# A four-stage block on one core: places of work chosen anew, own places for the first and last tile times, first layer and attention turns in column groups

## The reference

```python
x = layernorm(x + attention(x))      # 16 heads of 16, one shared key and value head, softmax over all 512
x = layernorm(x + ffn(x))            # 256 -> 1024 -> 256, weights ternary, exact gelu
x = layernorm(x + state_space(x))    # norm, B, cumulative sum with decay A, C, then the recurrence, then out_w
x = layernorm(x + linear(x))         # both operands quantised to fp6 in blocks of 32, 256 -> 256

def step(h, xt):                     # the recurrence, one step for each of 512 positions
    cat = concatenate([xt, h])
    ff1, ff2 = tanh(cat @ ff1_w.T + ff1_b), tanh(cat @ ff2_w.T + ff2_b)
    t_i = sigmoid((cat @ ta_w.T + ta_b) * 0.1 + (cat @ tb_w.T + tb_b))
    return ff1 * (1 - t_i) + t_i * ff2
```

## Time and profile before

| | before |
|---|---|
| median of 3 runs | 1768.9 us (1768.15 to 1773.33) |
| the profiled execution, its own time | 1771.39 us |
| its span | 1769.6 us |
| PE busy | 1637.5 us, 93% |
| DVE busy | 1343.4 us, 76% |
| ACT busy | 1293.2 us, 73% |
| POOL busy | 1104.3 us, 62% |
| matmuls | 35371 |
| PE's instruction queue | 280 packets, 4.59 MB |

### The profile page before, as it was taken

The page is one execution under the profiler, slowest core; times in us unless marked ns, Lnnn a source line. Parts: engine busy times, 40 slices in busy tenths (PEclk is TensorE's granted clock), DMA queues, the critical chain, the costliest instruction groups (busy, mean ns, idle before and its releaser), DMA issues.

```text
span 1769.6 us, 84556 instructions
## 1 busy us (share of the span) xinstructions
PE 1637.5 (93%) x35371; PEld 1189.0 (67%) x35371; DVE 1343.4 (76%) x2605; ACT 1293.2 (73%) x2601; POOL 1104.3 (62%) x3392
## 2 busy tenths in 40 slices
PE   5768999999999999999999999999999999999865
PEld 4535667677777777677777777777777767776643
...
GB/s 239 203 93 54 60 58 62 74 72 69 51 72 73 73 66 58 67 73 72 70 61 62 74 72 69 61 62 74 71 71 61 62 71 71 73 58 32 18 29 20
DMA packets 133765, 125.18 MB, mean 71 GB/s; under 512 B 18965, under 2 KB 130633, under 8 KB 133385
## 3 DMA queue, kind: packets, MB, share of 16 engines
...
...
## 4 chain that ended last, share of the span: by engine, by line
PE 53%; POOL 15%; ACT 10%; issue 8%; DVE 4%; DMA 4%; SPq 4%; POOLq 0%; DVEq 0%; ACTq 0%
PE value_bank L772 11%; PE gen_bank L910 8%; PE score_banks L750 7%; PE gen_bank L598 6%; PE max_banks L590 6%; PE gate_bank L803 5%; ACT L1130 4%; ACT probs L1130 3%; PE gen_bank L819 3%; PE gate_bank L598 2%; POOL square L1613 2%; POOL rstd L1598 2%; DMA key_pieces<-khalf 2%; POOL diff L1717 2%; POOL hseq L1722 2%
## 5 line engine op out<-in xcount | busy, mean ns | idle before, releaser
L1186 DVE TENSOR_REDUCE nmax<-max_banks 128x2 f32<-128x1024 f32 x512 | 622.5, 1216 | 65.3 <-PE max_banks L592 61.3
L1130 ACT ACTIVATE probs<-score_banks 128x1024 f32<-128x1024 f32 x512 | 525.0, 1025 | 112.3 <-PE score_banks L752 96.3
L772 PE MATMUL value_bank<-probs,vaug 128*32 128x128 f32 x8192 | 327.3, 278 | 1.1 <-issue 1.1
L772 PEld LDWEIGHTS value_bank<-probs,vaug 128*32 128x32 f32 x8192 | 205.5, 110 | 90.6 <-issue 79.7
L590 PE MATMUL max_banks<-kaug,qaug 62*128 62x512 f32 x512 | 238.7, 466 | 24.8 <-DVE nmax L1186 15.7
L750 PE MATMUL score_banks<-qaug,kaug 64*128 64x512 f32 x512 | 237.6, 464 | 12.4 <-ACT probs L1130 7.8
L1717 POOL TENSOR_TENSOR diff<-gates 128x16 f32<-128x16 f32 x472 | 114.2, 242 | 212.3 <-ACT gates L1135 205.1
L592 PE MATMUL max_banks<-kaug,qaug 62*128 62x512 f32 x512 | 239.2, 467 | 0.4 <-issue 0.4
L752 PE MATMUL score_banks<-qaug,kaug 64*128 64x512 f32 x512 | 237.6, 464 | 0.0
L1135 ACT ACTIVATE gates<-gate_bank 128x48 f32<-128x48 f32 x472 | 99.0, 210 | 167.6 <-PE gate_bank L803 167.2
L803 PEld LDWEIGHTS gate_bank<-hseq,ghT 128*32 128x32 f32 x11328 | 159.1, 112 | 81.3 <-POOL hseq L1722 57.4
(11 more groups left out here) (234 smaller groups left out, 3540.6 us busy)
## 6 DMA issues: line engine op xcount, KB each, us to landing
qstage<-qhalf SPq DMA_DIRECT2D x384, 128.0 KB
qstage<-qhalf SPq DMA_DIRECT2D x128, 112.0 KB
...
qaug<-nmT SPq DMA_DIRECT2D x256, 8.0 KB, 1.8
```

Source lines behind the costliest of these rows:

```text
L772: last = pe.matmul(value_bank[32 * g:32 * g + 32, :].rearrange("p (k t) -> p k t", k=HG)[:, :, u * BLOCK_POS:(u + 1) * BLOCK_POS], vaug[:, ...
L1130: act.activation(probs[:, beat % 2, :, :], score_banks[:, :, :], ACT.Exp).then_inc(exp_done, 1)
L1186: dve.tensor_reduce(nmax[:, m % 2, at:at + 9:8], max_banks[:, :, :], AX_X, ALU.max, negate=True).then_inc(max_taken, 1)
```

## The change

1. All slots of a steady tile time are other ones. On PE the order becomes: VALUES0, Q, STEP0, SCORES0, PAIR0, F2_0 to F2_7, TURND, SCORES1, PAIR1, XT, OT, STEP1, LAST, VALUES1, ATT, STEP2, PAIR2, SCORES2, PROJ, VALUES2, STEP3, SCORES3, PAIR3, VALUES3, OUT, STEP4, SCORES4, PAIR4, TURNX, VALUES4, SCORES5, VALUES5, STEP5, B, SCORES6, PAIR5, NM, X1T, STEP6, VALUES6, SCORES7, PAIR6, VALUES7, STEP7, FFN1A, FFN1B, PAIR7, INPUT (for the next tile time). On ACT: TANH0, Q, OT, EXP0, TURND, XT, TANH1, EXP1, ATT, TANH2, EXP2, TANH3, EXP3, TANH4, EXP4, X1, TURNX, EXP5, TANH5, EXP6, X1T, TANH6, X4, X2, EXP7, TANH7, GELUA, GELUB, Q8. On POOL HLOB stands ahead of XD, where it stood behind it.
2. Tile times -2 to 5 have places of their own (`OWN_AT`), and so has tile time 64 (`LAST_AT`). `tile_at`, `beat_at` and `times_of_uses` look there first.
3. `TAIL` and `TAIL_SSM` have other steps for X3B, QMAX, QSCALE, QIN, Q8, LN4, X4 and XN.
4. `QUARTERED` names the pieces whose matmuls are written in column groups. INPUT, LAST, Q, OUT, PROJ and B were so before. New are FFN1A and FFN1B (48 matmuls of 128 columns become 192 of 32) and ATT (2 transposes become 16 matmuls of 32 columns against the identity, written through `turned_block`).

The diff, cut to its core:

```diff
-PE_AT = dict(INPUT=0, F2_0=275, F2_1=280, F2_2=285, F2_3=285, F2_4=286, F2_5=288, F2_6=299, F2_7=302, TURND=279, LAST=322, XT=50, Q=12, OUT=128, OT=65, ATT=73, PROJ=90, TURNX=149, B=160, X1T=217, NM=204, FFN1A=247, FFN1B=249)
-ACT_AT = dict(OT=44, TURND=339, XT=104, Q=29, Q8=253, TURNX=196, ATT=145, X1T=230, GELUA=238, GELUB=239, X1=194, X2=178, X4=496)
-DVE_AT = dict(Q=23, X4R=362, X2R=52, OT=62, X3R=171, X3=239, QUANT=240, XN=148, LN1=157, BS=190, SCAN=236, ORDER=182, X1P=216, HLOA=240, NM=216)
-POOL_AT = dict(LN4=418, LN3=97, LN2=6, LNI=8, QIN=192, X2S=77, XD=214, X3B=193, LN1=15, X1B=116, STATES=165, HLOB=219)
-SP_AT = dict(MOVE=15, X2F=200, STORE=89, OUTST=406, XLD=59, NMPLACE=95)
+PE_AT = dict(INPUT=-2, F2_0=274, F2_1=275, F2_2=278, F2_3=278, F2_4=296, F2_5=297, F2_6=299, F2_7=304, TURND=309, LAST=336, XT=63, Q=8, OUT=134, OT=69, ATT=87, PROJ=100, TURNX=173, B=213, X1T=221, NM=217, FFN1A=240, FFN1B=247)
+ACT_AT = dict(OT=43, TURND=307, XT=51, Q=41, Q8=239, TURNX=158, ATT=99, X1T=193, GELUA=224, GELUB=236, X1=151, X2=202, X4=455)
+DVE_AT = dict(Q=27, X4R=371, X2R=85, OT=97, X3R=189, X3=205, QUANT=252, XN=141, LN1=145, BS=215, SCAN=238, ORDER=203, X1P=234, HLOA=260, NM=220)
+POOL_AT = dict(LN4=384, LN3=101, LN2=45, LNI=61, QIN=201, X2S=204, XD=222, X3B=200, LN1=96, X1B=217, STATES=154, HLOB=204)
+SP_AT = dict(MOVE=34, X2F=66, STORE=108, OUTST=365, XLD=46, NMPLACE=71)
 BEAT_AT = dict(
-    SCORES=(19, 61, 89, 107, 137, 157, 178, 231),
-    PAIR=(18, 55, 87, 102, 140, 202, 236, 250),
-    VALUES=(11, 68, 100, 128, 151, 157, 224, 252),
-    STEP=(15, 51, 72, 93, 135, 156, 166, 229),
-    EXP=(86, 121, 165, 181, 186, 227, 228, 236),
-    TANH=(46, 90, 125, 170, 181, 196, 227, 235),
-    MAX=(17, 26, 60, 107, 160, 190, 213, 233),
-    MIX=(3, 4, 12, 13, 20, 34, 96, 157),
+    SCORES=(14, 61, 99, 113, 154, 185, 216, 230),
+    PAIR=(14, 62, 97, 128, 168, 217, 230, 254),
+    VALUES=(3, 87, 111, 130, 180, 203, 227, 240),
+    STEP=(10, 74, 94, 112, 143, 209, 223, 240),
+    EXP=(49, 97, 121, 132, 142, 168, 179, 210),
+    TANH=(34, 66, 101, 128, 137, 174, 198, 224),
+    MAX=(15, 42, 96, 129, 165, 203, 216, 245),
+    MIX=(3, 61, 72, 80, 97, 109, 132, 133),
 )
-TAIL = dict(OUT=0, X3R=0, LN3=0, STATS3=1, X3=3, X3B=4, QMAX=4, QSCALE=5, QIN=6, Q8=7, XD=8, TURN=9, COPY=9, LAST0=10, LAST1=11, X4R=11, STATS4=12, LN4=12, X4=14, INPUT=1)
-TAIL_SSM = dict(F2=0, X2R=0, LN2=0, X2=2, X2S=2, XN=4, TURN=4, COPY=4, B=5, BS=5, SCAN=6)
+OWN_AT = {
...
+    -1: dict(
+        PE=dict(NM=142),
+        DVE=dict(NM=183),
+        SP=dict(NMPLACE=190),
+        BEAT=dict(PAIR=(-1, -1, -1, -1, -1, 36, 197, 211), MAX=(-1, -1, -1, -1, -1, -1, 12, 221)),
+    ),
...
+    5: dict(
+        PE=dict(INPUT=247, F2_0=80, F2_1=81, F2_2=83, F2_3=122, F2_4=124, F2_5=124, F2_6=126, F2_7=129, XT=140, Q=13, OT=140, ATT=154, PROJ=173, TURNX=190, B=219, X1T=206, NM=231, FFN1A=233, FFN1B=245),
+        ACT=dict(OT=13, XT=85, Q=13, TURNX=148, ATT=89, X1T=186, GELUA=238, GELUB=246, X1=125, X2=234),
+        DVE=dict(Q=51, X2R=82, OT=91, XN=113, LN1=130, BS=160, SCAN=216, ORDER=157, X1P=173, HLOA=26, NM=206),
+        POOL=dict(LN2=23, LNI=23, X2S=107, LN1=38, X1B=106, STATES=108, HLOB=248),
+        SP=dict(MOVE=1, STORE=18, XLD=4, NMPLACE=2),
+        BEAT=dict(SCORES=(22, 134, 141, 170, 184, 203, 219, 230), PAIR=(16, 136, 161, 179, 204, 225, 245, 246), VALUES=(13, 142, 160, 176, 189, 205, 223, 234), EXP=(17, 35, 51, 109, 111, 148, 200, 234), MAX=(39, 74, 103, 112, 142, 149, 201, 219)),
...
+LAST_AT = dict(
+    PE=dict(INPUT=254, F2_0=18, F2_1=19, F2_2=20, F2_3=23, F2_4=40, F2_5=41, F2_6=43, F2_7=48, TURND=53, LAST=80, OUT=134, OT=69, ATT=87, PROJ=100, TURNX=177, B=213, X1T=221, FFN1A=240, FFN1B=247),
+    ACT=dict(OT=42, TURND=90, Q8=239, TURNX=156, ATT=100, X1T=193, GELUA=224, GELUB=228, X1=136, X2=202, X4=199),
+    DVE=dict(X4R=100, X2R=70, OT=89, X3R=189, X3=205, QUANT=252, XN=146, LN1=145, BS=204, SCAN=238, X1P=194, HLOA=4),
+    POOL=dict(LN4=120, LN3=101, LN2=45, LNI=61, QIN=171, X2S=204, XD=222, X3B=215, LN1=96, X1B=213, STATES=212, HLOB=204),
+    SP=dict(X2F=154, STORE=156, OUTST=153),
+    BEAT=dict(VALUES=(3, 87, 101, 120, 170, 183, 202, 226), STEP=(0, 64, 89, 112, 121, 182, 221, 238), TANH=(24, 61, 101, 118, 122, 141, 173, 219), MIX=(3, 57, 73, 85, 98, 105, 130, 146)),
+)
+QUARTERED = ("INPUT", "LAST", "Q", "OUT", "ATT", "PROJ", "B", "FFN1A", "FFN1B")
+TAIL = dict(OUT=0, X3R=0, LN3=0, STATS3=1, X3=3, X3B=5, QMAX=5, QSCALE=6, QIN=7, Q8=8, XD=8, TURN=9, COPY=9, LAST0=10, LAST1=11, X4R=11, STATS4=12, LN4=11, X4=13, INPUT=1)
+TAIL_SSM = dict(F2=0, X2R=0, LN2=0, X2=2, X2S=2, XN=2, TURN=4, COPY=4, B=5, BS=5, SCAN=6)
...
+    tables = dict(PE=PE_AT, ACT=ACT_AT, DVE=DVE_AT, POOL=POOL_AT, SP=SP_AT)
+    def own(n):
+        return LAST_AT if n == TILES else OWN_AT.get(n, {})
+    def place(engine, name, n):
+        return own(n).get(engine, {}).get(name, tables[engine][name] % SLOTS)
+    def tile_at(engine, name, kind, n, at):
+        late = tables[engine][name] // SLOTS
         m = n - late + LEAD[kind]
-        return m if at == slot and live(m) and (kind not in ("X", "Q", "LOAD") or n - late >= 0) else None
-    def beat_at(name, at):
-        return BEAT_AT[name].index(at) if at in BEAT_AT[name] else None
+        return m if at == place(engine, name, n) and live(m) and (kind not in ("X", "Q", "LOAD") or n - late >= 0) else None
+    def beat_at(name, n, at):
+        slots = own(n).get("BEAT", {}).get(name, BEAT_AT[name])
+        return slots.index(at) if at in slots else None
...
-                slot = PE_AT[name] + SLOTS * (m - LEAD[kind])
+                n = m - LEAD[kind] + PE_AT[name] // SLOTS
+                slot = SLOTS * n + place("PE", name, n)
...
-            def in_quarters(out, weights, moving, start, stop):
+            def multiplied(name, out, weights, moving, start, stop):
+                if name not in QUARTERED:
+                    return pe.matmul(out(slice(0, P)), weights, moving, start=start, stop=stop, skip_group_check=True)
                 for q in range(0, P, 32):
-                    last = pe.matmul(out(q), weights[:, q:q + 32], moving, start=start, stop=stop, tile_position=(0, q), skip_group_check=True)
+                    last = pe.matmul(out(slice(q, q + 32)), weights[:, q:q + 32], moving, start=start, stop=stop,
+                                     tile_position=(0, q), skip_group_check=True)
                 return last
+            def turned_block(name, out, src):
+                if name not in QUARTERED:
+                    return pe.transpose(out(slice(0, P)), src, ident[:, :])
+                return multiplied(name, out, src, ident[:, :], True, True)
...
-                    last = pe.transpose(gen_bank[1][:, k * P:(k + 1) * P], xt[:, m % XR, k * P:(k + 1) * P], ident[:, :])
+                    last = turned_block("XT", lambda rows: gen_bank[1][rows, k * P:(k + 1) * P], xt[:, m % XR, k * P:(k + 1) * P])
...
-                    turn_tile(g0, att).then_inc(filled[0], 1)
+                    turn_tile("ATT", g0, att).then_inc(filled[0], 1)
...
-                                    last = pe.matmul(gen_bank[half][:, f * P:(f + 1) * P], w1Tb[:, k, (4 * half + f) * P:(4 * half + f + 1) * P],
-                                                     x1piece[:, piece, k, :], start=(piece + f + k == 0), stop=(piece == 2 and k == KT - 1),
-                                                     skip_group_check=True)
+                                    last = multiplied(("FFN1A", "FFN1B")[half], lambda rows: gen_bank[half][rows, f * P:(f + 1) * P],
+                                                   w1Tb[:, k, (4 * half + f) * P:(4 * half + f + 1) * P], x1piece[:, piece, k, :],
+                                                   piece + f + k == 0, piece == 2 and k == KT - 1)
...
```

More of the change, by code:

```diff
@@ L509, in mine @@
                     def mine(name, kind):
-                        return tile_at(SP_AT, name, kind, n, at)
+                        return tile_at("SP", name, kind, n, at)
                     m = mine("MOVE", "Q")
@@ L815, in general, with turn_tile @@
                 g0, g1 = gen_bank
[L817 removed]
+                def turn_tile(name, dst, src):
                     for k in range(KT):
[L819 removed]
+                        last = turned_block(name, lambda rows: dst[rows, k * P:(k + 1) * P], src[:, k * P:(k + 1) * P])
                     return last
                 def mine(name, kind):
[L823 removed]
+                    return tile_at("PE", name, kind, n, at)
                 m = mine("INPUT", "REC")
@@ L848, in general @@
                     for k in range(KT):
-                        last = in_quarters(lambda q: g1[q:q + 32, 0:D], xdT[:, k, :], wdT[:, k, :], k == 0, k == KT - 1)
+                        last = multiplied("LAST", lambda rows: g1[rows, 0:D], xdT[:, k, :], wdT[:, k, :], k == 0, k == KT - 1)
                     last.then_inc(filled[1], 1)
@@ L876, in general @@
```

(8 more changed lines are left out.)

94 lines of the change are left out of this document (68 added, 26 removed).

## The result

The changed kernel takes 1907.2 us (median of 4 runs, 1905.62 to 1911.91) against 1771.1 us of the kernel before on the same chips: 1.077 times as long, with a 95% interval of 1.0745 to 1.0802, or 136 us more. The span is 1904.6 us, 135 more than 1769.6.

What follows compares the result with a forecast made beforehand. PE's own order of work and its waits were taken to bound the kernel, then its instruction supply: 58 steady tiles x (26.0 - 24.52) = +86, early 0, tail -3, so 1771.4 + 83 = 1854 us; forecast 1800 to 1890, range 1750 to 1915.

Steps and rivals of the forecast that it cites:

- rival (3): Every instruction block costs 4.6 us and the clock adds to it; tile time 27.2, kernel 1923 us, chance 0.11.
- PE's own time: PE's work in a steady tile: 192 small first-layer matmuls at 13.9 ns take 2.66 us; tile sum 22.9 becomes 22.8.
- Supply, the mechanism: PE's instruction fetch: blocks of 256, two held, a new one asked for only when one is used up.
- Supply, the size: At 4.0 us a block, stalls of 3.4 us a tile, less 0.6 queued and 0.85 under waits: 1.95 left.
- The walk of the new order: A steady tile walked over five engines: 22.8 plus 1.25 of waits, 24.05 us, 0.47 better than 24.52.
- SCORES1's 0.6: PE waits 0.6 us a tile before SCORES1, as ScalarE's opening chain outlasts PE's 3.26 us of work.
- PROJ's wait "goes": The projection's wait of 0.38 us a tile goes, since LAST, VALUES1 and ATT stand between OT and PROJ.
- hlo and TURND behind xd: hlo is ready before the second layer, so its 0.24 us wait a tile goes, plus TURND's for xd.
- Ends: Early tile times 0, with 10 us either way; closing tile and steps -3, with 3 either way.
- (1): Rival: instruction supply does not bind, so the walk's gain holds; 1734 us, chance 0.17.
- (2): Rival: instruction supply binds mildly, 3.2 us a block; 1775 us, chance 0.12 shared with (4).
- (4): Rival: column groups do not bind, but the new order waits elsewhere, e.g. SCORES1 0.5 more; as (2), chance 0.12 shared.

Runs made afterwards that it cites:

- after_ffn_whole: The changed kernel with its first layer's 48 matmuls a tile of 128 columns again, all else kept; 1815.7 us, 1.023 times the kernel before.
- before_values2: The kernel before with VALUES2 ahead of PROJ instead of behind STEP3; 1792.3 us, 1.012 times the kernel before.
- before_hlo_first: The kernel before with HLOB ahead of XD, TURND moved on PE and ScalarE, and XT behind SCORES1, as in the new order; 1751.2 us, 0.988 times.
- after_mended: The changed kernel with first layer and ATT whole, VALUES7 behind PAIR7, STEP1 ahead of SCORES1, BS ahead of X3; 1771.6 us, 1.000 times the kernel before.
- after_whole_step1: As after_ffn_whole, with STEP1 ahead of SCORES1 on PE, where the old order had it; 1780.6 us, 1.005 times the kernel before.

## Why the prediction came out as it did

The direction and the cause that I put first held, and 1907 us lies in the range of 1750 to 1915. But it lies above the 1800 to 1890 that I gave to my own forecast, and nearer to rival (3)'s 1923 than to my 1854. Of 136 us I had 83; the 53 missing are about 1.06 us a tile: the order's walk 0.6, and the stalls hidden under waits 0.36 instead of 0.85. By its steps:

- **PE's own time: right.** 192 matmuls in 3.17 us for 48 in 3.14; 13.8 ns each in the mean over the changed kernel, without gaps of over 0.1 us, predicted 13.9. The 32-column bf16 loads take 97 ns, the 128-column ones took 99, so the price that I worked out beside the page "TensorEngine Tiling (Array Packing)" of the Trainium skill, section "Restrictions and Gotchas", did not come: whatever column tiling switches off there, no row here shows a loss by it.
- **Supply, the mechanism: right.** Blocks of 256, two in store, a fetch only at the boundary; the packets are 359, predicted about 360. The Trainium skill's page "Runtime: NRT & Kernel Launch", section "Instruction fetch mechanics", has the same blocks and two of them; its word that the fetch is hidden is not borne out, with 2.76 us of stalls a tile.
- **Supply, the size: the total by luck.** 3.4 - 0.6 = 2.8 us of stalls reckoned, 2.76 measured, but they are not the same ones. The block: taken 4.0, measured 3.76 and 3.85 where the DMA is quiet. Of its parts I had put the fetch at 1.0 although give 1.3; in the dense stretch the median is 1.0 for the fetch and 1.4 from its landing until PE goes on, and the next fetch begins about 1.3 us after that. The dense stretch: 2.8 us reckoned, 1.86 measured; no row gave the 0.6 in it that I let the queue ahead of the array hide, and no run shows that term by itself. Outside of the dense stretch: nothing reckoned, 0.90 measured, because I took the other 742 instructions as spread evenly ("256 in 5.7 us"). They are not: STEP1, LAST, VALUES1, ATT and STEP2 are 192 in one run, followed by PROJ, VALUES2 and STEP3, and that falls where the DMA is busy: the fetch ahead of a stall there takes 1.74 us in the median, in the dense stretch 1.0. STEP1 at its old place took the stalls outside from 0.81 to 0.44. And the 0.85 that I let stand "where PE would have waited anyway": the groups cost 1.55 us against 1.91 us of additional stalls in all, so the cover was 0.36, about Q's wait (VALUES0 to Q, without the stalls, 0.95 to 0.46 from start to start).
- **The walk of the new order: wrong by 0.6.** 24.05 us predicted; after_ffn_whole has 25.51, less its stalls of 0.85 that is 24.66. SCORES1's 0.6 was foreseen and came. In the changed kernel itself, where the stalls cover Q's wait, it is 24.3. Two waits were not seen. VALUES7 moved ahead of the first layer was costed at nothing; it had been the cover of GELUB, and Q waited 0.52 us. It gave something back there: the first layer's wait for the pieces of x1, which I had left in with 0.2 to 0.5, went (3.07 to 2.78). The 0.15 for B and STEP6 can't be seen: B takes 0.60 us for 0.62. NM waits 0.28 for BS, which has X3 ahead of it on VectorE; that is the sentence in which I costed the moves on DVE at nothing.
- **PROJ's wait "goes": right.** The row of waits says hardly, 24.1 us before and 18.3 after, but it is a wait of the load, which runs beside the matmuls ahead of it. From start to start PROJ went from 1.20 to 0.89 us. That such a gain need not reach the end is what before_values2 shows: there it was waited out again until STEP5, and the last operation of MIX came to lie beside VectorE's CAST.
- **hlo and TURND behind xd: right.** 0.24 us a tile from start to start, as in the rows. before_hlo_first is 0.30 us a tile shorter, 19 us in all, of which some 4 come behind the last NM; it has SCORES1, PAIR1 and PROJ shorter too and the recurrence later.
- **Ends:** early tile times -6.4 (0 with 10 either way), tail +1.5 (-3 with 3 either way): TURND's wait of 1.80 us did go, but the first layer stands 2.05 us for instructions there, and the second layer 0.58 for hlo.
- **The rivals.** (1) is out, (2) too; (4) holds in part, with SCORES1's 0.6 foreseen and Q and NM not. (3) had 1923, nearer to the time than I, but by blocks of 4.6 us each and the clock; blocks are 3.8 in quiet and only some elsewhere are longer. The clock's part is there and small. In the changed kernel's timeline, and then in its stretch from 346.50 to 351.00 us with the granted clock in the third number from the end:

```profile
345.91 0.24 PE L891 MATMUL gate_bank<-hseq,ghT 128*32 128x16 f32 x3 [2.05 <-issue]
346.08 0.76 PE L669 MATMUL max_banks<-kaug,qaug 62*128 62x512 f32 x1
```

```profile
346.50:351.00 4.50, 4.50 (x80) 2.48 (x82) 2.85 (x6) 1.74 (x3) 1.34 (x7) 0.66 0.18 37
...
342.50:1642.30 1299.80, 1152.30 (x33788) 856.71 (x33781) 988.30 (x1819) 934.71 (x1868) 814.22 (x2635) 0.99 0.38 62
```

PE fell to half speed for some us behind a stall of 2 us, as in the earlier trace rows; over the whole stretch the clock is 0.99 for 1.00.

The sum with the measured terms, from the changed kernel's own starts: stalls 2.76 - 0.20 = +2.56. Beside them the order's waits, SCORES1 +0.53, NM +0.30, STEP0 and ATT +0.15, and its gains, PROJ -0.31, the second layer and TURND -0.23, SCORES1 with PAIR1 -0.22, the first layer -0.17, come to nothing within 0.1: together +2.6 for +2.54. So the whole slowdown is as large as the stalls; the order's own gains and waits cancel.

Why after_mended ends at 24.75 us and the kernel before with hlo first at 24.22 is in the table of pieces: STEP7 waits 0.5 us longer for hseq (78.3 us on the load side, 29.3 in after_whole_step1), and SCORES1 and Q 0.3 and 0.2. No run tried an order in which other work covers one of the two.
